# A fused adaLN, Mamba and tree-FFN block: who makes du and dbu, and what stands in the table steps of ScalarE

## What is computed

```python
h = layernorm(x) * (1 + ca) + sa
xp, z = split(h @ W_in)                          # 256 channels each
u = silu(causal_depthwise_conv(xp))              # 4 taps
dt_r, Bm, Cm = split(u @ W_xp)                   # 8, 16, 16
delta = softplus(dt_r @ W_dt + dt_bias)
# for each of 16 states n and 256 channels e, over the tokens t:
h_t = exp(delta_t * A) * h_{t-1} + delta_t * Bm_t * u_t
y_t = sum_n h_t * Cm_t + u_t * D_skip
x = x + ga * ((y * silu(z)) @ W_out)
h = layernorm(x) * (1 + cb) + sb
gate = sigmoid((h @ Wq.T) @ routers.T)           # 255 nodes of a tree of depth 8
leaf_prob = product of branch probabilities      # 256 leaves
x = x + gb * ((leaf_prob @ leaf_values) @ Wout_w.T + Wout_b)
```

## Time and profile before

| | us |
|---|---|
| time, median of 3 runs | 494.99 |
| the 3 runs | 493.28 to 495.41 |
| the profiled execution's own time | 494.61 |
| its span, first to last instruction | 492.8 |
| VectorE busy | 450.6 |
| GpSimd busy | 430.3 |
| TensorE matmuls busy | 409.5 |
| ScalarE busy | 376.3 |

### The profile page before, as it was taken

The page is one execution under the profiler, slowest core; times in us unless marked ns, Lnnn a source line. Parts: engine busy times, 40 slices in busy tenths (PEclk is TensorE's granted clock), DMA queues, the critical chain, the costliest instruction groups (busy, mean ns, idle before and its releaser), DMA issues. The chain is left out here.

```text
span 492.8 us, 6755 instructions
## 1 busy us (share of the span) xinstructions
PE 409.5 (83%) x2172; PEld 278.1 (56%) x2172; DVE 450.6 (91%) x534; ACT 376.3 (76%) x689; POOL 430.3 (87%) x241
## 2 busy tenths in 40 slices
PE   7979766997599798997789798997899798688696
PEld 4436444674358456674648556664657456565374
DVE  5898899989999899989999889988999889999872
ACT  2467986598877898697977898698966897787825
POOL 4868899999999789988999899988999789999810
PEclk8989987998899989998999989998999988799999
DMA  6583036200831018300642018300642018300000
GB/s 177 151 312 138 1 107 260 87 0 1 289 121 45 1 39 330 108 0 2 234 164 77 2 41 328 107 1 0 240 161 76 0 42 326 107 2 21 0 23 21
DMA packets 23716, 51.06 MB, mean 104 GB/s; under 512 B 4474, under 2 KB 13825, under 8 KB 19585
## 3 DMA queue, kind: packets, MB, share of 16 engines
q1 hardware_dynamic: 23680, 50.64, 29.3%
HBM read 48.01 MB, written 2.62 MB: 103 GB/s over the span
## 5 line engine op out<-in xcount | busy, mean ns | idle before, releaser
L609 POOL TENSOR_TENSOR hc<-h,c_rows 128x1024 f32<-128x1024 f32 x127 | 298.3, 2367 | 26.8 <-DVE h L1368 26.7
L1368 DVE TENSOR_TENSOR_SCAN h<-dA,state,dbu 128x512 f32<-128x512 f32 x192 | 234.3, 1266 | 13.2 <-ACT dA L697 13.2
L697 ACT ACTIVATE dA<-delta,a_neg 128x512 f32<-128x512 f32 x256 | 173.2, 685 | 46.7 <-DVE h L1368 46.2
L1121 PEld LDWEIGHTS yb<-ident,hc 128*128 128x128 f32 x1024 | 130.0, 148 | 63.4 <-issue 43.7
L1121 PE MATMUL yb<-ident,hc 128*128 128x128 f32 x1024 | 154.0, 286 | 7.4 <-POOL hc L609 7.4
L1381 DVE TENSOR_TENSOR dbu<-du,bb 128x1024 f32<-128x1024 f32 x88 | 105.5, 1199 | 4.1 <-PE bb L1147 3.8
L596 POOL TENSOR_TENSOR dbu<-du,b_rows 128x1024 f32<-128x1024 f32 x40 | 94.6, 2366 | 3.9 <-DMA b_rows<-bc_dram 3.9
L1368 DVE TENSOR_TENSOR_SCAN h<-dA,dbu 128x512 f32<-128x512 f32 x64 | 74.2, 1206 | 5.5 <-ACT dA L697 5.4
L1147 PE MATMUL bb<-b_parts,sel 128*128 128x512 bf16 x88 | 35.1, 399 | 43.1 <-DVE dbu L1381 41.7
L1021 PE MATMUL mf<-f_hT,w_conv 128*128 128x512 f32 x112 | 55.1, 617 | 2.0 <-ACT zu L757 1.4
L1147 PEld LDWEIGHTS bb<-b_parts,sel 128*128 128x128 bf16 x88 | 8.7, 99 | 56.1 <-DVE dbu L1381 35.5
(11 more groups left out here) (206 smaller groups left out, 534.2 us busy)
## 6 DMA issues: line engine op xcount, KB each, us to landing
c_rows<-bc_dram SPq DMA_DIRECT2D x32, 1024.0 KB, 8.0
b_rows<-bc_dram SPq DMA_DIRECT2D x40, 256.0 KB, 9.4
xs<-in_L_attn_x_dram SPq DMA_DIRECT2D x8, 256.0 KB, 4.0
out_dram<-xs SPq DMA_DIRECT2D x7, 256.0 KB, 5.5
ygT<-in_L_attn_conv_w_dram SPq DMA_DIRECT2D x1, 512.0 KB, 5.7
bc_dram<-xd SPq DMA_DIRECT2D x8, 64.0 KB, 1.6
probT<-in_L_wmod_dram SPq DMA_DIRECT2D x1, 384.0 KB, 4.6
w_in<-in_L_attn_W_in_dram SPq DMA_DIRECT2D x1, 256.0 KB, 4.4
```

What stands on the lines that cost most here:

```text
L609: nc.gpsimd.tensor_tensor(hc[:, pair % RC, :, :], h[:, pair % RH, :, :], c_rows[:, q, n % NQ, :].unsqueeze(1).broadcast_to([P, HALVES, T]) ...
L697: nc.scalar.activation(dA[ke % RD][:, :], delta[:, ge % 2, half, :], ACT.Exp, scale=a_neg[:, half, n:n + 1]).then_inc(s_dA, 1)
L1121: last = nc.tensor.matmul(bank[:, tile], hc[:, pair % RC, half, tile], ident[:, :], start=False, stop=n == N - 1 if last_of_bank is None e ...
L1368: v.tensor_tensor_scan(h[:, pair % RH, half, :], dA[k % RD][:, :], dbu[:, pair % RW, half, :], start, ALU.mult, ALU.add).then_inc(s_scan, 1)
```

## The change

- POOL_N becomes (2, 5, 7, 9, 11, 14): GpSimd makes six dbu of a group, states 7 and 9 instead of 8, and VectorE ten. SP loads six b_rows tiles a group.
- The two du of groups 1 to 7 are made by VectorE, at step F_DU = 19 behind the dbu of that step, instead of by GpSimd.
- A function made_at gives the pair that is filled and made at a step. It takes state 12 out of its turn (step 22) and puts it at step K_EARLY = 19, the fill on TensorE too.
- The front statistics of step 19 stand ahead of the dbu.
- The silu step moves from step 10 to 11, the tail statistics from 14 to 13, the `dt` products one step later each.
- ScalarE's copies of `out` and `ff` move, within a step, from behind the softplus step and the copy of `yt` to ahead of the silu step. `out` is still read at step 11, which is now the silu step.

```diff
@@ -73,18 +73,19 @@
     PAIRS = K // HALVES
     RB, RY, RD, RH, RC, RW = 1, HALVES, 3, 4, 4, 4
     RM = {"f": 1, "t": 1}
-    POOL_N = (2, 5, 8, 11, 14)
+    POOL_N = (2, 5, 7, 9, 11, 14)
     NB = len(POOL_N)
     AHEAD_POOL = 3
     AHEAD_EXP, AHEAD_FILL, AHEAD_DBU, LAG_SUM = 2, 3, 2, 5
+    N_EARLY, K_EARLY = 12, 19
 
 
 
 
     N_STATS, N_RSTD, N_OFF, N_XHAT = 19, 2, 3, 6
-    F_SILU, F_SP, F_DU = 10, 17, (25, 26)
+    F_SILU, F_SP, F_DU = 11, 17, 19
     F_HI, F_R1, F_MID, F_R2, F_LO = 21, 22, 23, 24, 25
-    T_GATE, T_STATS, T_RSTD, T_OFF, T_XHAT = (4, 5), 14, 19, 20, 24
+    T_GATE, T_STATS, T_RSTD, T_OFF, T_XHAT = (4, 5), 13, 19, 20, 24
     NORMS = {2: (4, 3)}
     NORMS.update({g: (g + 1, g) for g in range(4, GROUPS)})
 
@@ -93,8 +94,8 @@
 
     JOBS = {
         "f": {("xp", 0): (1, (0, 1)), ("xp", 1): (1, (3, 4)), ("z", 0): (1, (7,)), ("z", 1): (1, (8,)),
-              ("dt", 0): (1, (11, 12)), ("xd", 0): (1, (18, 19)), ("tr", 0): (2, (28,))},
-        "t": {("yt", 0): (-1, (6,)), ("yt", 1): (-1, (8,)), ("out", 0): (-1, (10,)), ("dt", 1): (1, (13, 14)),
+              ("dt", 0): (1, (12, 13)), ("xd", 0): (1, (18, 19)), ("tr", 0): (2, (28,))},
+        "t": {("yt", 0): (-1, (6,)), ("yt", 1): (-1, (8,)), ("out", 0): (-1, (10,)), ("dt", 1): (1, (14, 15)),
               ("lp", 0): (-2, (19,)), ("lp", 1): (-2, (21,)), ("ff", 0): (-2, (23, 24)), ("tr", 0): (-1, (27,)),
               ("node", 0): (-1, (29,)), ("node", 1): (-1, (30,))},
     }
@@ -382,6 +383,15 @@
 
             return pair // N * NB + sum(n < pair % N for n in POOL_N)
 
+        def made_at(k, ahead):
+
+            g, n = divmod((k + ahead) // HALVES, N)
+            if k >= 0 and k % STEPS == K_EARLY:
+                return k // STEPS * N + N_EARLY
+            if (k + ahead) % HALVES == 0 and 0 <= k + ahead < K and n not in POOL_N and n != N_EARLY:
+                return g * N + n
+            return None
+
         def by_dve(pair):
 
             return pair - by_pool(pair)
@@ -608,12 +618,6 @@
                             pool.wait_ge(s_sum, HALVES * (pair - RC + 1))
                         nc.gpsimd.tensor_tensor(hc[:, pair % RC, :, :], h[:, pair % RH, :, :], c_rows[:, q, n % NQ, :].unsqueeze(1).broadcast_to([P, HALVES, T]),
                                                 ALU.mult).then_inc(s_hc, 1)
-                    if front and s in F_DU:
-                        half = F_DU.index(s)
-                        wait_delta(pool, f, half)
-                        pool.wait_ge(s_silu, f + 1)
-                        nc.gpsimd.tensor_tensor(du[:, f % 2, half, :], delta[:, f % 2, half, :],
-                                                zu[:, f % 2, HALVES + half, :], ALU.mult).then_inc(s_du, 1)
 
         @block.scalar
         def _(act):
@@ -756,6 +760,12 @@
                                 act.wait_ge(s_gate, HALVES * (f - 2) + half + 1)
                             nc.scalar.activation(zu[:, f % 2, half, :], job("f", "z", half, f)[1][:, :],
                                                  ACT.Copy).then_inc(s_read["f"], 1)
+                    for name in ("out", "ff"):
+                        for g2 in due(name, 0, g, s):
+                            wait_job(act, "t", name, 0, g2)
+                            nc.scalar.activation(xs[:, g2 * TILES:(g2 + 1) * TILES, :],
+                                                 job("t", name, 0, g2)[1][:, :].rearrange("p (i d) -> p i d", d=DM),
+                                                 ACT.Copy).then_inc(s_read["t"], 1)
                     if g >= 0 and s == F_SILU:
                         if front:
 
@@ -812,12 +822,6 @@
 
                             wait_job(act, "t", "yt", half, t)
                             nc.scalar.activation(ygT[:, half, :], job("t", "yt", half, t)[1][:, :],
-                                                 ACT.Copy).then_inc(s_read["t"], 1)
-                    for name in ("out", "ff"):
-                        for g2 in due(name, 0, g, s):
-                            wait_job(act, "t", name, 0, g2)
-                            nc.scalar.activation(xs[:, g2 * TILES:(g2 + 1) * TILES, :],
-                                                 job("t", name, 0, g2)[1][:, :].rearrange("p (i d) -> p i d", d=DM),
                                                  ACT.Copy).then_inc(s_read["t"], 1)
                     if due("tr", 0, g, s):
                         wait_job(act, "t", "tr", 0, t)
@@ -1131,9 +1135,9 @@
                 front = 1 <= f < GROUPS
                 for s in range(STEPS):
                     k = g * STEPS + s
-                    kf, ks = k + AHEAD_FILL, k - LAG_SUM
-                    if 0 <= kf < K and kf % HALVES == 0 and kf // HALVES % N not in POOL_N:
-                        pair = kf // HALVES
+                    ks = k - LAG_SUM
+                    pair = made_at(k, AHEAD_FILL)
+                    if pair is not None:
                         gf, n = divmod(pair, N)
                         if n == 0:
                             pe.wait_ge(s_lo, gf + 1)
@@ -1367,9 +1371,10 @@
                         start = state[:, n, half:half + 1] if g % CHUNKS else 0.0
                         v.tensor_tensor_scan(h[:, pair % RH, half, :], dA[k % RD][:, :], dbu[:, pair % RW, half, :],
                                              start, ALU.mult, ALU.add).then_inc(s_scan, 1)
-                    kd = k + AHEAD_DBU
-                    if 0 <= kd < K and kd % HALVES == 0 and kd // HALVES % N not in POOL_N:
-                        pair = kd // HALVES
+                    if 4 <= g + 4 < GROUPS and s == N_STATS:
+                        stats(g + 4, f_bn, f_mv[:, g + 4, :, :], s_fvar)
+                    pair = made_at(k, AHEAD_DBU)
+                    if pair is not None:
                         gd, n = divmod(pair, N)
                         if n == 0:
                             dve.wait_ge(s_du, HALVES * (gd + 1))
@@ -1381,8 +1386,12 @@
                         v.tensor_tensor(dbu[:, pair % RW, :, :], du[:, gd % 2, :, :],
                                         bb[mine % RB][:, :].unsqueeze(1).broadcast_to([P, HALVES, T]),
                                         ALU.mult).then_inc(s_dbu, 1)
-                    if 4 <= g + 4 < GROUPS and s == N_STATS:
-                        stats(g + 4, f_bn, f_mv[:, g + 4, :, :], s_fvar)
+                    if 1 <= f < GROUPS and s == F_DU:
+                        dve.wait_ge(s_silu, f + 1)
+                        for half in range(HALVES):
+                            wait_delta(dve, f, half)
+                            v.tensor_tensor(du[:, f % 2, half, :], delta[:, f % 2, half, :],
+                                            zu[:, f % 2, HALVES + half, :], ALU.mult).then_inc(s_du, 1)
                     if tail and s in T_GATE:
 
                         half = T_GATE.index(s)
```

## The result

The changed kernel takes 513.89 us (median of 4 runs, 511.97 to 514.13), beside 494.13 for the kernel before on the same chip (4 runs, 493.23 to 495.41): a ratio of 1.0386, 95% interval 1.0362 to 1.0409. It is slower by 19.8 us, where 513.0 was forecast. The profiled execution took 511.97, with a span of 510.2.

A forecast was written before the change was run, and what follows sets the result against it. VectorE, busy 91%, sets the pace. Groups 2 to 6 add 13.5 us, group 1 3.1, group 0 about 2, group 7 0: +18.6 on 494.6 gives 513.2, taken as 513.0; own range 507 to 517, 8 in 10 498 to 518.

The forecast's parts named there:

- The sum: Whole kernel: group 0 about +2 us, group 1 3.1, groups 2 to 6 2.7 each, group 7 0; together +18.6.
- The silu step: Table step at 11: ScalarE's out copy idles 1.8 us for TensorE, VectorE's wait goes from 1.4 to 3.3; +1.8 us.
- The softplus step: Between scans 19 and 20: first du waits 1.1 us (2.3 in groups 4 to 6) for hc 9; scan 20 +3.9 us.
- The 1.72 us of the earlier trace: First half of VectorE's very last hc, read as waiting for GpSimd's running hc; the second half took 0.69 us.
- a sign of being wrong: Forecast wrong if out's copy starts without idle, all du measure 0.69 us, or a wait for b_rows or bb appears.
- Rival 1: Softplus step: no conflict, du take 0.69 us whatever GpSimd does; 13.4 us less, 500; chance 0.13.
- Rival 3: Both table steps: du unhindered and out's copy not waited for, so VectorE's waits shrink; 489; chance 0.09.
- Rival 2: Silu step: out's copy not waited for, TensorE being sooner; 1.8 us less in six groups, 502; chance 0.08.

The follow-up runs named there:

- e3: Changed kernel with the out product making only one of its four token tiles in groups 0 to 6, order kept: 506.92 us, ratio 1.0243.
- b1: Kernel before with only the fill and the dbu of state 12 moved to step 19, behind the front statistics: 495.80 us, ratio 1.0033.
- b3: Kernel before with only the two du moved to VectorE at step 19, behind the front statistics; GpSimd keeps five dbu: 510.58 us, ratio 1.0317.
- b5: Kernel before with only the two du moved to VectorE, at step 20, behind scan 20: 503.14 us, ratio 1.0185.
- c1: Changed kernel with du on GpSimd, copies of out and ff behind, silu at step 10, dt at 11 to 14: 503.40 us, ratio 1.0177.
- e7: Changed kernel with copies of out and ff behind the table steps, tail statistics at 14, and du on GpSimd at steps 25 and 26: 501.99 us, ratio 1.0143.
- e4: Changed kernel with du ahead of step 19's dbu, reading PSUM bank bb instead of u, so another product is computed: 506.83 us.
- e5: Changed kernel with the two du ahead of the dbu of state 12 instead of behind it, still reading delta and u: 520.99 us.
- e2: Changed kernel with the two du given back to GpSimd at steps 25 and 26: 509.28 us, ratio 1.0306.
- b4: Kernel before with only the dbu of state 9 moved from step 16 to step 12, its fill to step 13: 503.35 us, ratio 1.0169.
- b6: Kernel before with only the tail statistics moved from step 14 to step 18: 495.07 us (10 runs) beside 494.57, ratio 1.0001.
- e1: Changed kernel with copies of out and ff back behind the silu and softplus steps, tail statistics at step 14: 508.96 us, ratio 1.0298.

## Why the prediction was right

**The sum.** Between the profiled executions the last hc of VectorE moved from 473.34 to 490.11, +16.8, forecast +18.6; the rest of the 17.4 is in the closing part. By groups, from scan 28 to scan 28: groups 2 to 6 gave 2.64, 2.75, 2.30, 2.61 and 2.63, together 12.9 where 5 x 2.7 was forecast; group 1 2.56 (3.1), group 0 1.16 (2), group 7 0.1 (0). The 0.5 in group 1 were an overestimate. The 0.84 missing in group 0 are the opening of the kernel before, which ran 1.5 us long in its profiled execution for a low clock of TensorE (last section); beside an opening without it group 0 gives some 2.6. The profiled execution was the fastest of the four, 1.9 us under their median, 513.89.

**The silu step.** Right in groups 1 to 6: ScalarE's copy waited 1.80 to 1.90 us (forecast 1.8), VectorE 3.25 to 3.35 (3.3; 3.71 in group 4). e3 showed that the copy's wait is VectorE's, one to one. In group 0 the gain to scan 19 was 1.78, where 1.7 by scan 17 was forecast, but that is luck: 1.5 of it is the long opening of the kernel before. From the first scan to scan 19 the changed kernel took 32.54 us, and b1, b3 and b5, with the old code up to there, 33.07, so the change gains only 0.5. The worth of the later step by itself, put at 0.6, does not show either (c1 and e7).

**The softplus step.** Right in groups 1 to 6: 1.88 and 0.68 us for the two du in group 3, ending 0.54 behind hc 9 (forecast 0.55), no wait ahead of scan 20. The 1.72 us of the earlier trace rows was no accident; e4 and e5 showed its cause. Two things were missed. In group 0 the two du were to wait in full, 2.95 us each, and took 2.15 and 0.94. And VectorE did wait for bb at dbu 12, 0.84, 0.66 and 0.66 us in groups 4 to 6, which the forecast had named as a sign of being wrong. It cost nothing, since the du behind it had hc 9 to wait for anyway: they took 2.28 to 2.33 us there and ended 0.54 to 0.55 behind it.

**What was wrong are prices of rivals.** Rival 1, no conflict, was put at 500, 13.4 us less; e4 is near that kernel (its product is another one) and takes 506.8, 7.1 less. Rival 3, no conflict and no wait for the copy, was put at 489; e7, which undoes both by other means, takes 502.0. Both were priced as if VectorE kept all that it gains. The step missed is one that ScalarE's timeline before would have shown: in group 3, from dA 20 to 28, ScalarE idles 0.4 us in 12 (one wait for TensorE), and dA 28 was only 0.3 to 0.4 us early. A loss on VectorE ahead of that stretch counts in full, a gain does not. The forecast was on the side of the losses, where this does not show. Rival 2, no wait for the copy, at 502, was priced about right: e3 takes 1.35 of the 1.8 us away in six groups, 8.1 by that price, and gave 7.0. Part of the rest is group 1, where its du pair met two hc in a row (1.25 and 2.83 us).

**Chances.** The change was held slower at 0.85, on two terms of which each would have been enough: b3 has the du alone and is slower by 3.2%, and e2 has the copy without the du and is slower by 3.1%. But 1.4% are left with both undone (e7), by the traces above all for the choice of states. To that the forecast gave no loss of its own: it was in the sum, since the walk along VectorE's instructions had dbu 8 in it, and not among the reasons.

## What to carry to other kernels

As far as these runs go, time here is a chain of stretches, each with its own owner: table steps and what follows them are ScalarE's, the rest VectorE's. Work moved from one wait into another gives nothing (b4), nor does work taken out of a stretch that the other engine owns (b1). Only work taken out of a stretch that the engine itself fills counts, the next stretch must have room for it (e2), and a group that lacks the wait must not pay for it (b6). Before an instruction with a wait goes ahead of a table load, ask when its product is there, since everything behind the table waits with it; and before an elementwise product of two SBUF tensors goes to VectorE, look at what GpSimd runs at that moment, as a step later may cost 1.2 us instead of 2.5 to 4.9.

## What was not expected of the hardware

- In the changed kernel, e1, e3, e5, b3 and b5 a VectorE du that started while an hc of GpSimd ran ended 0.54 to 0.56 us behind it, in 48 of 50 cases (0.61 in the other two), and an hc that started while a du ran was itself longer, 2.79 to 2.86 instead of 2.37 us; two du in a row took up to 4.89 us so (e5). A GpSimd operation of 0.20 us took 0.58 beside a du (b5).
- The opening differs between executions by 1.5 to 1.7 us, and TensorE's clock makes it. From the first scan to scan 13 of group 0 the kernel before took 25.60 us, and b1, b3, b5 and b6, with the same code there, 24.11 each; e2 took 22.75, and six kernels with its code there 21.06 each. In the kernel before, e2 and c1 the mean granted clock from 32 to 36 us was 0.57 to 0.60, so TensorE was for a part of it at the lower of its two levels, 1.2 GHz; in all others it was 1.00, that is 2.4 GHz. The same eight matmuls in the kernel before (with the wait of VectorE) and in b6:

```profile
32.17 5.19 PE L1021 MATMUL mf<-f_hT,w_conv 128*128 128x512 f32 x8 [1.44 <-ACT zu L757]
...
37.62 1.22 DVE L1381 TENSOR_TENSOR dbu<-du,bb 128x1024 f32<-128x1024 f32 x1 [1.15 <-PE bb L1147]
```

```profile
31.28 3.70 PE L1021 MATMUL mf<-f_hT,w_conv 128*128 128x512 f32 x8 [1.44 <-ACT zu L757]
```

They take 1.49 us longer, the fill of bb stands behind them, and VectorE waits 1.15 us for it, where in b6 it does not wait. A difference below 2 us between two single executions can come from this alone.
